# Gated cross-attention and top-1 expert block on one core: the attention pipeline's lags shortened by one slot, maxima turned in another slot, routing in fewer slots

## The reference, cut to what matters

```
x = x + tanh(g_xattn) * xattn(layernorm(x), ctx, ctx)      # x, ctx: 128 x 64 x 128; 16 heads of 8
x = x + tanh(g_ffn)  * ffn(layernorm(x))

xattn: q = LN(x) Wq + bq; k = ctx Wk + bk; v = ctx Wv + bv
       probs = softmax(q k^T / sqrt(8)) over 64 keys, per head; out = (probs v) Wo + bo
ffn:   logits = (x w_red) wg_n^T            # 8 experts
       e = argmax(softmax(logits)); score = max(softmax(logits))
       h = gelu(x W1[e] + b1[e]);  o = (h W2[e] + b2[e]) * score
```

## Time and profile before

| | |
|---|---|
| median of 3 runs | 363.32 us (363.27 to 365.42) |
| the profiled execution | 366.57 us, its span 364.8 us |
| PE busy | 314.0 us (86%) |
| DVE busy | 286.6 us (79%) |
| POOL busy | 268.1 us (73%) |
| ACT busy | 240.4 us (66%) |
| chain that ended last | PE 44%, POOL 17%, DVE 16%, issue 8%, ACT 8% |
| costliest groups on POOL | output scatters 70.0 us (x71), record sends 63.5 us (x64), normed rows 44.4 us (x56) |

### The profile page before, as it was taken

The page is one execution under the profiler, slowest core; times in us unless marked ns, Lnnn a source line. Parts: engine busy times, 40 slices in busy tenths (PEclk is TensorE's granted clock), DMA queues, the critical chain, the costliest instruction groups (busy, mean ns, idle before and its releaser), DMA issues.

```text
span 364.8 us, 15361 instructions
## 1 busy us (share of the span) xinstructions
PE 314.0 (86%) x5630; PEld 237.8 (65%) x5630; DVE 286.6 (79%) x1031; ACT 240.4 (66%) x604; POOL 268.1 (73%) x349
## 2 busy tenths in 40 slices
PE   3879899999998999999998977865987999999950
PEld 1526657766775676676675655644966999999840
DVE  7675798889899999999898998877677666666630
ACT  3653889989898888998989964544433555555520
POOL 6482963684796898998899877587657777777771
PEclk9965999999999999999999996796799999999995
DMA  5344255334322423224212121162124433433210
GB/s 115 102 135 130 83 124 145 93 110 109 119 68 87 149 76 115 92 73 127 66 53 80 49 73 51 43 163 68 49 78 120 141 111 109 118 103 96 67 40 0
DMA packets 47157, 34.01 MB, mean 93 GB/s; under 512 B 9800, under 2 KB 42955, under 8 KB 47083
## 3 DMA queue, kind: packets, MB, share of 16 engines
q1 hardware_dynamic: 42440, 23.90, 23.1%
q0 software_dynamic: 4352, 9.00, 7.4%
q10 hardware_dynamic: 292, 0.13, 0.2%
HBM read 17.13 MB, written 10.04 MB: 74 GB/s over the span
## 4 chain that ended last, share of the span: by engine, by line
PE 44%; POOL 17%; DVE 16%; issue 8%; ACT 8%; SPq 2%; DMA 1%; POOLq 0%; DVEq 0%; ACTq 0%
PE m L1344 10%; PE sc L1254 9%; POOL records L403 6%; POOL xn L378 4%; PE sc L1132 4%; DVE mx L987 3%; PE m L1306 3%; PE pv L1207 3%; PE pv L1213 2%; ACT PT L601 2%; PE sc L1142 2%; PE sc L1125 2%; PE sc L1246 2%; PE m L1341 2%; ACT PT L599 2%
## 5 line engine op out<-in xcount | busy, mean ns | idle before, releaser
L987 DVE TENSOR_REDUCE mx<-sc 128x8 f32<-128x512 f32 x128 | 82.3, 684 | 18.0 <-PE sc L1142 17.7
L474 POOL DMA_INDIRECT out<-fo,rr x71 | 70.0, 986 | 23.1 <-issue 19.3
L403 POOL DMA_INDIRECT records<-XR,pos x64 | 63.5, 993 | 19.2 <-issue 16.2
L599 ACT ACTIVATE PT<-sc 128x512 f32<-128x512 f32 x64 | 38.1, 596 | 24.6 <-issue 19.2
L1344 PE MATMUL m<-w,fgT 128*128 x284 | 50.7, 302 | 0.1
L1254 PE MATMUL sc<-fxT,w1s 128*128 128x128 f32 x284 | 45.9, 286 | 4.5 <-DVE w1s L975 3.8
L1058 DVE SCALAR_TENSOR_TENSOR fo<-m,rr 128x128 f32<-128x128 f32 x71 | 24.9, 350 | 29.9 <-PE m L1344 29.9
L1207 PE MATMUL pv<-PT,V 128*32 128x64 f32 x2048 | 43.6, 227 | 5.4 <-DVE XR L999 4.8
L378 POOL TENSOR_SCALAR xn<-XC,mv,rstd 128x128 f32<-128x128 f32 x56 | 44.4, 802 | 0.0
L1254 PEld LDWEIGHTS sc<-fxT,w1s 128*128 128x128 f32 x284 | 39.0, 199 | 6.5 <-ACT fxT L581 4.2
L581 ACT ACTIVATE fxT<-sc 128x128 f32<-128x128 f32 x71 | 19.7, 277 | 34.8 <-PE sc L1246 34.8
(11 more groups left out here) (208 smaller groups left out, 700.7 us busy)
## 6 DMA issues: line engine op xcount, KB each, us to landing
rr<-records SPq DMA_DIRECT2D x71, 72.0 KB, 1.9
XC<-in_x SPq DMA_DIRECT2D x16, 256.0 KB, 4.0
C<-in_ctx SPq DMA_DIRECT2D x16, 256.0 KB, 3.9
Qd<-Qf SPq DMA_DIRECT2D x64, 64.0 KB, 1.9
Kd<-kb SPq DMA_DIRECT2D x64, 32.0 KB
w<-in_L_ffn_W SPq DMA_DIRECT2D x16, 128.0 KB, 2.7
out<-fo,rr POOLq DMA_INDIRECT x71, 2.3
w1l<-in_L_ffn_W SPq DMA_DIRECT2D x8, 128.0 KB, 3.9
```

Source lines behind the costliest of these rows:

```text
L403: nc.gpsimd.indirect_dma_start(out=records, out_offset=bass.IndirectOffsetOnAxis(ap=pos[:, u:u + 1], axis=0), in_=XR[:, u, :], in_offset=N ...
L474: nc.gpsimd.indirect_dma_start(out=out_rows, out_offset=bass.IndirectOffsetOnAxis(ap=rr[q][:, R_ID:R_ID + 1].bitcast(U32), axis=0), in_=fo ...
L599: nc.scalar.activation(pt[:, 0:2], sc[:, 0:2, 256:512], ACT.Exp)
L987: nc.vector.tensor_reduce(mx[c % 2][:, t:t + 2, HI * u:HI * u + HI], sc[:, t:t + 2, 0:256].rearrange("p t (i k) -> p t i k", i=HI), AX_X, ...
```

## The change

The four lags go from 4, 10, 11, 12 to 3, 9, 10, 11, so the loop has 75 slots in place of 76. The transpose of a chunk's maxima and their copy move from the slot with j = 0 to the one with j = 3 in front of it. The routing steps of a group are closer together and earlier, the last three parts of `whole_tiles` stay in slots 66 to 68. The table of sends is as it was.

```
-LAG1, LAG2, LAGV, LAGO = 4, 10, 11, 12
+LAG1, LAG2, LAGV, LAGO = 3, 9, 10, 11
...
     if g <= LISTED:
-        return r + 12, r + 13, r + 14, r + 17, r + 18, r + (19 if g < LISTED else 18)
+        return r + 11, r + 12, r + 12, r + 13, r + 16, r + 17
     if g < LAST - 1:
-        return r + 11, r + 12, r + 12, r + 13, r + 14, r + 14
-    return r + 11, r + 11, r + 11, r + 12, r + 12, r + 13
+        return r + 10, r + 11, r + 11, r + 12, r + 13, r + 13
+    return r + 10, r + 10, r + 10, r + 11, r + 11, r + 12
...
 (scalar)
-                if j == 0 and 2 <= s < NC + 2:
-                    act.wait_ge(mT_ps, s - 1)
-                    if s >= 4:
-                        act.wait_ge(md_ok, s - 3)
-                    nc.scalar.activation(mS[s % 2][:, :], m2[:, 0:P], ACT.Copy, scale=-1.0).then_inc(mS_ok, 1)
                 if j == 3 and 1 <= s < NC + 1:
                     act.wait_ge(xw_ps, s)
+                    act.wait_ge(mT_ps, s)
+                    if s >= 3:
+                        act.wait_ge(md_ok, s - 2)
+                    nc.scalar.activation(mS[(s - 1) % 2][:, :], m2[:, 0:P], ACT.Copy, scale=-1.0).then_inc(mS_ok, 1)
...
-                if k == 10:
+                if k == 9:
                     output_logits()
...
 (vector)
-                for part, at in enumerate((listed, listed + 1, listed + 5, listed + 6, listed + 7)):
+                for part, at in enumerate((listed, listed + 1, listed + 9, listed + 10, listed + 11)):
...
 (tensor)
                 if j == 3 and 1 <= s < NC + 1:
                     x_logits(s - 1)
+                    pe.wait_ge(mx_ok, CU * s)
+                    nc.tensor.transpose(m2[:, 0:P], mx[(s - 1) % 2][:, :, :].rearrange("p t r -> p (t r)"),
+                                        ident[:, :]).then_inc(mT_ps, 1)
...
                     nc.tensor.transpose(m2[:, 2 * P:3 * P], xwT[:, :], ident[:, :]).then_inc(xwt_ps, 1)
-                    pe.wait_ge(mx_ok, CU * (s - 1))
-                    nc.tensor.transpose(m2[:, 0:P], mx[s % 2][:, :, :].rearrange("p t r -> p (t r)"),
-                                        ident[:, :]).then_inc(mT_ps, 1)
```

## The result

The changed kernel took 389.15 us (median of 4 runs, 384.81 to 392.56); the kernel before, beside it, 363.94 us (4 runs). The ratio is 1.0638, 95% interval 1.0559 to 1.0717: slower, as forecast, but by 25 us where 16 had been worked out, and outside the range of 369 to 386. The ratios in this document are taken over the faster executions of each kernel, here without 390.97 and 392.56 us, and so differ a little from the ratio of the medians. The profiled execution is the fastest of the four, 384.81 us with a span of 383.1, 18.2 us above the profiled execution of before.

The account below looks back on a forecast made before the run. POOL was taken as the bound from 114.5 us on, at a fixed distance from its norm of chunk 9; 13.1 us of lateness plus 3 for the clock, 16.1 on the median 363.32, gave 379 us, range 369 to 386.

Parts of the forecast that it names:

- The bound: From 114.5 us on, the end stands at a fixed distance from POOL's norm of chunk 9, but for idle times.
- the step on chunks 9 to 15: Loop with sends: 13.65 to 13.75 us a chunk against POOL's 13.01, so POOL no longer bounds; 4.5 us more.
- The wait for the copies: First scores of each chunk's first tile wait for the four key copies: 0.9 us a chunk, all on the path.
- The turn of the maxima: Slot 63: ACT's copy of chunk 14's maxima, behind the values' copies, ends 1.5 us later; no price in each chunk.
- Prologue: Early slots and chunks 2 to 7: +1.7, +1.7, +0.9 and +5.4 us, making slot 33 9.7 us late.
- The spread maxima: Slot 37 waits for MD of chunk 7 and starts 3.76 us later by this alone; slot's work 13.5 us late.
- The end: Last maxima come in slot 67, not 68; POOL's idle 2.62 us goes, leaving +13.1 us; closer routing frees nothing.
- The clock: Behind slot 37's wait of about 2.9 us, PE's clock drops to 0.50 for 10 us: +3 us.
- The sum of 16.1 us: Whole kernel: 13.1 us of lateness at the end plus 3 us for the clock drop, on the median 363.32.
- a rival with 0.17: Repeated drops: where copies land late PE idles 1.4 us and more; two further low stretches of 3 us, 385 us; chance 0.17.

Follow-up runs that it names:

- the run with first scores alone: The kernel before with LAG1 = 3 and nothing else, so first scores come one slot sooner: 379.34 us, ratio 1.0492.
- The halved copies: The kernel before with LAG1 = 3 and each of the four key copies issued as two of half the columns: 436.02 us, ratio 1.2025.
- the turn alone: The kernel before, lags unchanged, with the maxima's transpose and ScalarE's copy mS moved to a chunk's fourth slot: 369.45 us, ratio 1.0194.
- the run with the first scores back and the biases split later: The changed kernel with LAG1 = 4 again and VectorE's split of the output biases two slots later: 381.92 us, ratio 1.0444.
- the first scores back: The changed kernel with LAG1 = 4 again, all else as changed: 384.9 us, ratio 1.0618.
- the run with three groups back: The changed kernel with the routing of its first three groups at the old distances: 390.13 us, ratio 1.0721.
- the last chunk's: The kernel before with the turn and copy mS of chunk 15 alone in slot 67, not 68: 363.95 us, ratio 1.0013.

## Why the prediction was partly right, step by step

**The bound: right in the traces, not confirmed by the times, gone after.** From MD of chunk 15 to the start of the last output scatter it is 123.0 to 128.1 us in the traces of undisturbed chips (before 124.2, changed 124.0). But in the one run that moved this MD alone, 3.3 us sooner, the time stayed the same. And POOL's stretch with sends was no longer continuous, as the step on chunks 9 to 15 said.

**The wait for the copies: the mechanism right, its size nearly.** 0.9 us a chunk was forecast; the run with first scores alone has 0.69 us on the median fourth slot and 9.1 us of waits in all. The halved copies show the wait on the path. In the changed kernel only 7.6 us of it are seen, where 10 or more had been forecast; that other lateness covers the rest is argued. What the waits cost is more than their length (11.6 us for 8.1 in the loop of the run with first scores alone).

**The turn of the maxima: the step that failed.** The prediction gave it a price only once, at the end ("ACT's copy of chunk 14's maxima ... ends 1.5 us later"), and none in each chunk: in the step on chunks 9 to 15 it kept the 8.6 us from the first scores of a chunk's fourth slot to the end of the next keys, a stretch that now holds the turn. Its median over chunks 2 to 14 is 8.7 us before, 9.2 with the turn alone and 9.3 in the changed kernel. The other part of its sum, from the keys to the first scores, came out: 4.15 + 0.9 = 5.05 us was forecast, the median is 4.9. Alone the turn makes the fourth slot 0.43 us longer and the kernel 7 us slower, and 7 us on top of 379 would have been 386, the edge of the range. The error was to let the transposition cost what it cost in slot 4c, and not to ask how old the maxima are that it reads: there a slot, here none.

**Prologue: the sum too small.** +9.7 us was forecast for slot 33; the keys of chunk 8, in that slot, end 12.3 us later (125.57 against 113.32). A chunk from 2 to 7 was to take 13.6 us, and four of the six steps from the second to the seventh lie at 14.4 us or below; the third and seventh are 17.1 and 15.8. The third is a collision of VectorE and GpSimd that no row of before shows; the run with the first scores back and the biases split later puts 4 us on it. The seventh holds a second one, the product L1008 beside GpSimd's subtraction (rows in the last section). In the nine traces with such a product of 1.3 us or more in the seventh step, all of kernels with the later lags, that step is 15.5 to 16.0 us long; in the three of the later lags without it 14.4 to 14.7. No run moves this collision by itself, so its price of some 1.3 us is argued. The terms of the sum for the first slots (19.27 and 1.3 + 0.4 + 1.2 + 0.4) give 22.6 us and not "about 23.0", 0.4 us less.

**The spread maxima: right in another kernel.** Slot 37 was to wait 2.9 us for MD. In the changed kernel it starts 0.4 us behind the end of that MD and doesn't wait:

```profile
131.78 0.32 PE L1141 MATMUL sc<-Kd,qb 32*64 32x256 bf16 x8 [1.99 <-issue]
...
135.71 0.40 PE L1124 MATMUL sc<-MD,usel 32*128 32x256 bf16 x4
...
139.42 0.29 PE L1124 MATMUL sc<-MD,usel 32*128 32x256 bf16 x4 [0.25 <-ACT PT L601]
```

```profile
138.38 0.63 POOL L446 TENSOR_TENSOR MD<-mS,imask 128x256 bf16<-128x256 bf16 x1
```

The slots ahead were late by themselves: the copies' wait of 1.99 us at slot 35, and the clock behind it. With the first scores back the wait was there, 3.42 us long. As forecast, the ninth step is a long one (16.7 us), but for the other reason: that the two have like sizes is luck. Slot 37 was to start at 123.82 + 13.5 = 137.3 us.

**Chunks 9 to 15: mis-sized.** 13.65 to 13.75 us each was forecast; from the keys of chunk 9 to those of chunk 15 it took 85.9 us, 14.3 each (13.1 before). Of the missing 0.6 us a chunk the turn has 0.4. The rest goes with the later scores' sooner slots (slots 1 and 3 of the table, 0.31 and 0.21 longer than before, slot 2 0.22 shorter), where TensorE waits longer for exponentials (16.9 us between 36 and 230 us, 7.6 before between 36 and 212). MD of chunk 14 was to be 15.7 us late and is 21.2.

**The end: right.** The 2.62 us of idle time went, MD of chunk 15 has no wait, and the 21.2 became 18.4. Routing freed nothing, as far as the run with three groups back shows.

**The clock: right in kind, not in place or size.** 3 us for one low stretch of 10 us behind slot 37 was taken. The profiled execution has one of 3.4 us, from 133.4 us on, behind the copies' wait at slot 35, and one of 6.8 in the prologue; that of before had 17.1 us in the prologue (from 20.3 us on) and 10.2 from 221.7 on. The four executions of the changed kernel lie at a mean granted clock of 0.955, 0.951, 0.942 and 0.925 and take 384.81, 387.34, 390.97 and 392.56 us. The sum of 16.1 us is near the 18.2 of the profiled pair, in part by luck: the prologue and chunks 9 to 15 were too small by 2.6 and 2.8 us, and the end gave back 4.5 us (from 22.9 us late at the keys of chunk 15 to 18.4 at its MD). Of the other 7 us, 4.3 are that this execution was the fastest of the changed kernel, and 2.6 that the one of before lay above its median.

Stretches of the changed kernel behind slot 35's wait (order of columns as above):

```profile
129.00:133.00 4.00, 1.96 (x62) 1.50 (x62) 1.43 (x5) 1.59 (x5) 3.92 (x6) 1.00 0.18 62
133.00:137.00 4.00, 4.00 (x70) 3.22 (x69) 2.42 (x10) 2.25 (x4) 3.21 (x4) 0.57 0.39 124
```

The Trainium skill (TensorE: Matmul & The Clock Gate, HAM oscillation) describes a loop that falls to the low clock whenever it waits for a transfer. In the prediction this was a rival with 0.17; by the run with halved copies it is what happens here when each wait is 2.7 us or longer (twelve of thirteen). In the changed kernel's loop one wait for the copies of three between 1.1 and 2.0 us had a low stretch behind it.

**What makes the whole.** In hundredths of the time before: the turn costs 1.9, the first scores 4.9 alone and 3.9 on top of the turn, and the later lags with the routing 4.2 on top of the turn but 0.6 on top of both. The last two each suffice for most of the loss, and cover each other. Each ratio has an interval of 0.7 to 1.0 either way, and the kernels ran on different chips, so the 0.6 may be 0 or 2. Why the later lags cost so much is shown in part: one collision (4 us) by an edit, a second (some 1.3 us) only by the steps it goes with; a 3.42 us wait for MD has the low clock behind it, but taking it away moved the loss to the next step. The later lags without the turn were not run.

## What to carry to other kernels

When a step is moved to a sooner place in a loop, ask for each of its inputs how old it was in the old place and how old it will be in the new one: an operation that costs 0.1 us where its input is a slot old cost some 0.4 us where it is fresh, in every round. A wait in a loop of dependent engines (scores, maxima, exponentials, next scores) can cost more than its length: here 8.1 us of waits came with 11.6 us of loss, and 38.7 us of them with 59, with the low clock behind many of them. Where causes cover each other, undoing one shows little; do each alone on the kernel before as well, and only then call one the cause or rule it out.

## What the runs showed of the hardware

**Short VectorE operations can be held for as long as GpSimd is busy.** A CAST of 8 columns took 2.90 us in the changed kernel, and 0.12 to 0.32 us elsewhere. It ended when GpSimd's row of memsets, 0.1 to 0.5 us each, did:

```profile
42.41 2.90 DVE L801 CAST bhl<-bw 128x8 bf16<-128x8 f32 x1
45.35 0.17 DVE L802 TENSOR_TENSOR br<-bw,bhl 128x8 f32<-128x8 f32 x1
```

```profile
42.24 1.27 POOL L370 TENSOR_TENSOR XR<-XC,tgbo 128x512 f32<-128x512 f32 x1
43.44 0.21 POOL L418 MEMSET tri<- 128x128 bf16 x1
...
45.19 0.10 POOL L426 MEMSET ebase<- 128x1 f32 x1
```

A product of VectorE (L1008, median 0.29 us) took 2.44 us beside GpSimd's subtraction:

```profile
103.76 2.44 DVE L1008 TENSOR_TENSOR NV<-TV,rec 128x128 f32<-128x128 f32 x1
```

```profile
103.70 2.36 POOL L395 TENSOR_TENSOR w<-w,w1l 128x1024 f32<-128x1024 f32 x1
```

All 128 reductions and 128 transpositions of the loop kept their times (646 to 693 ns, 287 to 313 and 423 to 450). The Trainium skill (SBUF — State Buffer, Who interferes with whom) says that VectorE and GpSimd share a port pair as an exclusive lock, that casts can enter a mode that takes it, that operations with two inputs in SBUF contend with what GpSimd reads there, that reductions don't contend, and that the later one blocks until the other's instruction is done. The trace agrees on which kinds were held; but this CAST was held over more than one instruction of GpSimd, from 42.41 to 45.31 us. With the biases split two slots later the CAST took 0.12 us: a shift between the two engines can make or remove a 3 us stall that no row of the old trace hints at.

**The clock follows single waits, but not all of them.** In eleven traces of undisturbed chips (all but that of the kernel before, the last chunk's and the halved copies with sooner scores) there are 33 waits of TensorE of 1.3 us or longer between 40 and 225 us; with 21 of them a stretch of 3.4 or 6.8 us at the low level (0.50, 1.2 GHz) begins, from 0.4 us before the wait's end to 1.8 us behind it. It was so for all four waits of 2.7 us or longer, and for 17 of the 29 shorter ones. Between 40 and 216 us the kernel before has no such wait, and no low stretch.

**Issuing has its own price.** Eight copies of half the size took 4.92 us to issue in place of 2.38, for the same bytes.
